# Two heads side by side in the first attention, half products, an early first load, and earlier bank hand-over in the second attention

## The reference, cut to what matters

```
first half:  n = layernorm(x); q, k, v = n @ W + b, with low-rank additions (16 heads of 16)
             routed experts: 32 experts (128 -> 128 -> 128, relu squared), 8 chosen per token, and a
             shared expert of 512; their gate gives g
first attention, per batch of 1024 tokens and per head of 16:
             softmax(q k^T / 4) v      (all 1024 keys), then @ Wo + bo; x1 = g * that + x
gate network: a ternary-weight gated network on layernorm(x1)
second attention, 32 heads of 64, rotary positions: 30 local heads (blocks of 128 queries on 192 keys,
             causal), 2 causal heads over all 1024; @ Wo + bo; times g2, plus x1
```

## Time and profile before

| | |
|---|---|
| median of 3 runs | 3305.22 us (3304.18 to 3305.37) |
| the profiled execution's own time | 3307.49 us |
| its span in the trace | 3305.7 us |
| mean granted TensorE clock | 0.982 |
| TensorE busy | 3098.8 us (94%) |
| weight loads | 2208.1 us (67%) |
| VectorE busy | 2139.0 us (65%) |
| ScalarE busy | 1854.7 us (56%) |
| POOL busy | 1111.6 us (34%) |

### The profile page before, as it was taken

The page is one execution under the profiler, slowest core; times in us unless marked ns, Lnnn a source line. Parts: engine busy times, 40 slices in busy tenths (PEclk is TensorE's granted clock), DMA queues, the critical chain, the costliest instruction groups (busy, mean ns, idle before and its releaser), DMA issues. The chain is left out here.

```text
span 3305.7 us, 62515 instructions
## 1 busy us (share of the span) xinstructions
PE 3098.8 (94%) x21586; PEld 2208.1 (67%) x21586; DVE 2139.0 (65%) x6393; ACT 1854.7 (56%) x4670; POOL 1111.6 (34%) x1753
## 2 busy tenths in 40 slices
PE   7999999979999999996987999999999999999998
PEld 5888888822333333333776888788877888778886
DVE  5776666658888888874755555555556555555555
ACT  4666666627767767673445555455554555445553
POOL 1111111010010010002015556575555655566554
PEclk9999999979999999997999999999999999999999
DMA  4111111042223132101324434354343443244432
GB/s 137 42 41 43 40 44 37 15 83 38 51 47 67 27 71 42 29 8 55 132 75 107 98 89 96 92 121 97 79 113 86 112 98 89 65 112 101 97 83 65
DMA packets 310379, 241.68 MB, mean 73 GB/s; under 512 B 150768, under 2 KB 256688, under 8 KB 309936
## 3 DMA queue, kind: packets, MB, share of 16 engines
q1 hardware_dynamic: 310064, 237.69, 29.2%
HBM read 100.71 MB, written 39.85 MB: 43 GB/s over the span
## 5 line engine op out<-in xcount | busy, mean ns | idle before, releaser
L1660 ACT ACTIVATE b_pp<-b_pp,b_nm 128x192 f32<-128x192 f32 (+2 forms) x1024 | 472.5, 463 | 458.5 <-DVE b_nm L1828 377.0
L903 DVE TENSOR_REDUCE a_mx<-ps 128x1 f32<-128x512 f32 x1024 | 636.5, 681 | 88.3 <-PE ps L851 88.2
L825 ACT ACTIVATE a_pt<-ps 128x512 f32<-128x512 f32 x1024 | 534.9, 601 | 245.1 <-PE ps L862 243.6
L1630 POOL TENSOR_SCALAR b_pp<-b_pp,b_rc 128x192 f32<-128x192 f32 x960 | 388.0, 430 | 441.1 <-DVE b_rc L1837 441.1
L1849 DVE COPY b_pt<-ps 128x384 f32<-128x384 f32 (+2 forms) x336 | 182.0, 555 | 388.1 <-PE ps L1749 369.7
L851 PE MATMUL ps<-a_k,a_q 96*128 96x512 bf16 x1024 | 399.3, 391 | 18.9 <-DMA a_k<-qk_parts 16.1
L862 PE MATMUL ps<-a_q,a_k 99*128 99x512 bf16 x1024 | 387.4, 382 | 8.9 <-issue 5.4
L1828 DVE CUSTOM_DVE_ANT_0 b_pp<-ps,b_mk 128x192 f32<-128x192 f32 x960 | 276.3, 353 | 130.8 <-PE ps L1728 130.8
L638 DVE SCALAR_TENSOR_TENSOR f_yac<-ps,f_cw,f_yac 128x128 f32<-128x128 f32 x992 | 276.6, 343 | 122.2 <-PE ps L447 120.7
L851 PEld LDWEIGHTS ps<-a_k,a_q 96*128 96x128 bf16 x1024 | 100.1, 98 | 292.1 <-issue 152.6
L447 PEld LDWEIGHTS ps<-w,f_sq 128*128 128x128 f32 x2048 | 264.9, 191 | 29.7 <-DVE f_yac L638 7.2
(11 more groups left out here) (254 smaller groups left out, 7104.3 us busy)
## 6 DMA issues: line engine op xcount, KB each, us to landing
b_rt<-b_qf SPq DMA_DIRECT2D x1024, 64.0 KB, 2.0
qk_parts<-f_aa SPq DMA_DIRECT2D x32, 384.0 KB, 2.6
a_q<-qk_parts SPq DMA_DIRECT2D x192, 64.0 KB, 3.0
a_k<-qk_parts SPq DMA_DIRECT2D x96, 128.0 KB, 5.2
v_rows<-f_va_ SPq DMA_DIRECT2D x16, 512.0 KB, 3.0
a_v<-v_rows SPq DMA_DIRECT2D x4, 2048.0 KB, 11.6
b_raw<-in_W1qT SPq DMA_DIRECT2D x64, 128.0 KB, 2.6
b_raw<-in_W1kT SPq DMA_DIRECT2D x64, 128.0 KB, 2.8
```

What stands on the lines that cost most here:

```text
L825: e.activation(pt[(4 * i + j) % 8][:, :], P.ap(s), ACT.Exp).then_inc(P.free_sem(s), 1)
L903: e.tensor_reduce(mx[kh % 3][:, j * 4 + t, h:h + 1], P.ap(s), AX.X, ALU.max, negate=True).then_inc(P.free_sem(s), 1)
L1630: m = e.tensor_scalar(x, x, r[:, 2 * u + h:2 * u + h + 1], 1.0, ALU.mult, ALU.mult)
L1660: e.activation(x, x, ACT.Exp, bias=nm[n % 4][:, c:c + 1], scale=-1.0, accum_out=sm[n % 4][:, c:c + 1]).then_inc(exp_done, 1)
```

## The change

- In the first half q and k are stored as two fp32r parts (high, low): ScalarE writes the high part with the bias, VectorE makes the low part from the bank. POOL has no part in it.
- In the first attention two heads lie side by side: one head's three stacked parts (48 rows) from partition 0, the next head's from partition 64. `max` becomes a pair of products into two neighbouring banks, read by one reduction; 32 a unit. `score` becomes a pair of products too. The maximum is added by two extra rows, made by VectorE alone. Four row transfers instead of three.
- Banks: pairs 0-1 and 2-3 for maxima and all side steps, 4 to 6 for scores, 7 for the weighted sums. There are 12 `pt` tiles.
- `pv` is split in two halves of 256 columns, of which the second is issued half a position later. Step `two` is emptied by VectorE instead of ScalarE.
- The ones in the k tiles come by six transfers. Unit 0 is loaded in the first half's last chunk, into the space of experts 0 to 15 (`ahead` step of the first half); the values have a load step of their own.
- In the second attention banks 0 and 2 are handed on at the fourth of the eight maxima. For the last batch VectorE does the gating in place of POOL.

```diff
+
+    def pair(self, step):
+        i = self.at[step][0]
+        return self.ps[:, i:i + 2, :]
...
+                if (c, e) == (NCH - 1, 14):
+                    p.append(("ahead",))
...
-                    w.wait_ge(aa2_done, m + 1)
+                    w.wait_ge(*P.emptied(("qk", c, s[2])))
                     dst = X["qk"][n, :, h * 128:(h + 1) * 128, c * CH:(c + 1) * CH].rearrange("s p t -> p s t")
-                    e.dma_start(dst, aa[m % 2][:, :, :]).then_inc(aa_out[m % 2], 16)
+                    e.dma_start(dst, aa[m % 2][:, :, :].bitcast(F32)).then_inc(aa_out[m % 2], 16)
...
+                elif k == "ahead":
+
+                    w.wait_ge(*P.filled(("up", NCH - 1, 15)))
+                    for i in range(2):
+                        w.wait_ge(aa_out[i], 16 * 2 * 2)
+                    load_unit(e, X, 0, M["q0"], M["k0"], M["q0_in"], M["k0_in"])
...
-                    w.wait_ge(r1_done, m - 1)
-                    e.activation(qf[m % 2][:, :], P.ap(s), ACT.Identity,
-                                 bias=M["bqk"][:, n, h:h + 1]).then_inc(P.free_sem(s), 1)
+                    w.wait_ge(aa_out[m % 2], 16 * (m // 2))
+                    e.activation(aa[m % 2][:, 0, :], P.ap(s), ACT.Identity,
+                                 bias=M["bqk"][:, n, h:h + 1]).then_inc(aa_high, 1)
...
-                    e.tensor_copy(aa[m % 2][:, 1, :], r1[m % 2][:, :]).then_inc(aa1_done, 1)
+                    n, h, m = s[2] // 2, s[2] % 2, 4 * c + s[2]
+                    w.wait_ge(aa_high, m + 1)
+                    e.scalar_tensor_tensor(out=aa[m % 2][:, 1, :], in0=P.ap(s), scalar=M["bqk"][:, n, h:h + 1],
+                                           in1=aa[m % 2][:, 0, :].bitcast(F32), op0=ALU.add,
+                                           op1=ALU.subtract).then_inc(P.free_sem(s), 1)
...
@@ first_attention_plan()
             emitted += 1
-            if emitted % 32 == 0:
-                out.append(("both", emitted // 32 - 1))
-                late.append((slot + (2 if slot else 0), ("rows", emitted // 32 - 1)))
+            if emitted % 16 == 0:
+                out.append(("both", emitted // 16 - 1))
+                late.append((slot + (1 if slot else 0), ("rows", emitted // 16 - 1)))
         return out
 
     p += ahead(0)
     while late:
         p.append(late.pop(0)[1])
...
+            if (u + 2) % 4 == 0:
+                p.append(("load_v", (u + 2) // 4))
+        p += ahead(2 * i + 1)
+        if i + 1 < 16 * units:
+            p.append(("score", i + 1, 0))
+        if c:
+            p.append(("pv", i - 1, 1))
+        if 2 <= c <= 5 and side:
+            p.append(side.pop(0))
+        p += ahead(2 * i + 2)
+        if i + 1 < 16 * units:
+            p.append(("score", i + 1, 1))
+        p.append(("pv", i, 0))
         if c == 7:
-            p.append(("evac", i // 8))
+            p += [("pv", i, 1), ("evac", i // 8)]
             if u % 4 == 3:
                 if i + 1 == 16 * units:
                     p += side
@@ -701,48 +706,67 @@
                 f0 = 8 * (u // 4) + 4 * h
                 for n in range(6):
                     side += [(s, f0 + n - lag) for lag, s in ((2, "three"), (1, "two"), (0, "one")) if 0 <= n - lag < 4]
-        elif 2 <= c <= 5 and side:
-            p.append(side.pop(0))
     return p + side
 
...
+    b, g = n // 4, n % 4
+    for m, parts in ((1, (0, 0, 1)), (0, (0, 1, 0))):
+        for h in range(2 if m == 0 else 1):
+            for a in range(2):
+                for r in range(3):
+                    rows = slice(64 * a + 16 * r, 64 * a + 16 * r + 16)
+                    src = X["qk"][m, parts[r], g * 64:(g + 1) * 64, b * L:(b + 1) * L].rearrange(
+                        "(p a d) t -> a d p t", p=2, a=2)[a]
+                    if m:
+                        e.dma_start(k[rows, :, :].bitcast(F32), src).then_inc(k_in, 16)
+                    else:
+                        e.dma_start(q[rows, h, :, :].bitcast(F32), src[:, :, h * CH:(h + 1) * CH]).then_inc(q_in[h], 16)
...
@@ first_attention()
             if s[0] == "max":
-                P.take(s, s[1] % 3)
+                P.take(s, 2 * (n_max % 2), 2 * (n_max % 2) + 1)
+                n_max += 1
             elif s[0] == "score":
-                P.take(s, 3 + (4 * s[1] + s[2]) % 3)
-            elif s[0] == "pv":
-                group = s[1] // 8
-                if s[1] % 8 == 0:
-                    P.take(("group", group), 6 + group % 2, fills=False)
+                for a in range(2):
+                    P.take((*s, a), 4 + n_score % 3)
+                    n_score += 1
+            elif s[0] == "pv" and s[1] % 8 == s[2] == 0:
+                P.take(("group", s[1] // 8), 7, fills=False)
             elif s[0] == "last":
                 last = 0
                 if last is None:
-                    P.take(s, 6 + (1 - group % 2 if ("group", 0) in P.at else 0))
+                    P.take(s, 2 * (n_max % 2), 2 * (n_max % 2) + 1)
+                    n_max += 1
...
+        pt = [sb(f"pt{i}", [128, CH]) for i in range(12)]
...
             w = Waits(e)
+            w.wait_ge(one_set, 1)
+            for x in ks:
+                for a in range(2):
+                    dst = x[64 * a + KS:64 * a + KX, :, :].rearrange("r j (n t) -> r (j n) t", t=128)
+                    e.dma_start(dst.bitcast(F32), spread(one[:, :], 1, 16).bitcast(F32)).then_inc(ones_in, 16)
             for s in plan:
...
+                        w.wait_ge(*P.filled(("score", 16 * (n - 3) + 15, 1, 1)))
+                    if n:
+                        load_unit(e, X, n, qs[i], ks[i], q_in[i], k_in[i])
+                elif k == "load_v":
+                    if n >= 2:
+                        w.wait_ge(pv_done, pv_at[64 * (n - 1) - 1, 1])
+                    e.dma_start(vs[n % 2][:, :, :, :].rearrange("p i h d -> p i (h d)"),
+                                X["v"][n * L:(n + 1) * L, :].rearrange("(i p) f -> p i f", p=128)).then_inc(v_in[n % 2], 16)
                 elif k == "rows":
                     i, h = n // 2 % 3, n % 2
...
+                    w.wait_ge(*P.emptied(s))
+                    for a in range(2):
+                        for r in range(2):
+                            dst = qs[i][64 * a + KS + r:64 * a + KS + r + 1, h, :, :]
+                            e.dma_start(dst.rearrange("a p (t q) -> a (p t) q", q=128).bitcast(F32),
+                                        n2[n % 2][8 * a:8 * a + 8, r, :].bitcast(F32)).then_inc(rows_in[i][h], 16)
...
                     i, j = s[1], s[2]
-                    w.wait_ge(*P.filled(s))
-                    w.wait_ge(pv_done, i - 1)
-                    e.activation(pt[(4 * i + j) % 8][:, :], P.ap(s), ACT.Exp).then_inc(P.free_sem(s), 1)
+                    if i >= 3:
+                        w.wait_ge(pv_done, pv_at[i - 3, 1])
+                    for a in range(2):
+                        w.wait_ge(*P.filled((*s, a)))
+                        e.activation(pt[(4 * i + 2 * j + a) % 12][:, :], P.ap((*s, a)),
+                                     ACT.Exp).then_inc(P.free_sem((*s, a)), 1)
                 elif k == "evac":
...
-                    e.matmul(P.ap(s), q6[u % 3][0:KS, half, j, t * 128:(t + 1) * 128],
-                             k6[u % 3][0:KS, j, h * CH:(h + 1) * CH], start=True, stop=True).then_inc(P.full_sem(s), 1)
+                    for a in range(2):
+                        r = slice(64 * a, 64 * a + KS)
+                        m = e.matmul(P.pair(s)[:, a, :], qs[u % 3][r, half, j, t * 128:(t + 1) * 128],
+                                     ks[u % 3][r, j, h * CH:(h + 1) * CH], start=True, stop=True)
+                    m.then_inc(P.full_sem(s), 1)
...
+                        w.wait_ge(*P.before((*s, a)))
+                    for a in range(2):
+                        r = slice(64 * a, 64 * a + KX)
+                        e.matmul(P.ap((*s, a)), ks[u % 3][r, j, c * 128:(c + 1) * 128], qs[u % 3][r, h, j, :],
+                                 start=True, stop=True).then_inc(P.full_sem((*s, a)), 1)
...
+                    x = slice(256 * half, 256 * half + 256)
                     for j in range(4):
-                        w.wait_ge(*P.emptied(("score", n, j)))
-                        m = e.matmul(P.ap(group)[32 * j:32 * j + 32, :], vs[b % 2][:, c, 4 * g + j, :],
-                                     pt[(4 * n + j) % 8][:, :], start=c == 0, stop=c == 7)
+
+                        w.wait_ge(*P.emptied(("score", i, j // 2, j % 2)))
+                        m = e.matmul(P.ap(group)[32 * j:32 * j + 32, x], vs[b % 2][:, c, 4 * g + j, :],
+                                     pt[(4 * i + j) % 12][:, x], start=c == half == 0, stop=c == 7 and half == 1)
                     m.then_inc(pv_done, 1)
...
-                    e.tensor_reduce(mx[kh % 3][:, j * 4 + t, h:h + 1], P.ap(s), AX.X, ALU.max,
+                    e.tensor_reduce(mx[kh % 3][:, :, jt, h], P.pair(s), AX.X, ALU.max,
```

(16 more changed lines are left out.)

172 lines of the change are left out of this document (59 added, 113 removed).

## The result

The changed kernel takes 3195.8 us in the median of four runs (3188.35 to 3204.24), the kernel before 3305.3 on the same chip: a ratio of 0.967, 95% interval 0.9645 to 0.9695. That is 110 us less, where 174 were forecast (3131). It lies inside the range given for 8 in 10 (3085 to 3215), but outside the forecast's own branch (3090 to 3180), and most of one term of the sum is missing. The profiled execution took 3204.24 us, its span is 3202.4, its mean granted clock 0.977.

The account below looks back on a forecast made before the run. TensorE's order of work was taken to bound the first attention, VectorE close behind. Gains of 96 + 15 + 60 + 3 = 174 us off 3307.5 gave 3133.5, as a median 3131; range for 8 in 10: 3085 to 3215.

Parts of the forecast that it names:

- Second attention: Projections' wait on the eighth maximum (65.3 us) goes when two banks are freed at the fourth: 60 us less, bounds 45 to 72.
- Start: Start of first attention: unit 0 loaded earlier, first score about 700.2 instead of 716.04; gain 15 us, 8 to at most 17.
- End: Last eight tiles: VectorE gates faster than POOL, 0.8 us less on each of four turns, 3 us.
- First half: q/k steps lose VectorE and POOL passes, but TensorE is the bound there: nothing, within 2 us either way.
- The loop: First attention: 2.74 us a position against 3.125 over 244 positions, 94 us, plus 2 for the last 12: 96 less.
- Pair of products: First attention: two heads' products overlap on TensorE, 0.25 us a pair, bounds 0.23 to 0.46; four pairs 1.00 a position.
- the first rival: First attention: pairs run one after the other at 0.46 us, 3.54 a position; 3327 us in all, slower; 9%.
- A half sum: First attention's weighted sum of 256 columns: 0.44 us streaming plus 0.21 entering and leaving, 0.65; bounds 0.55 to 0.75.
- The three score banks in twos: First attention: a score pair needs the previous pair's first exponential; 1.1 us a half position, under 1.3.
- Side steps, rows and coupling: First attention: 0.285 us a position for output projection and row maxima steps, plus 0.11 for TensorE's wait at "rows".
- The clock: Granted clock holds at 1.00 in the first attention's loop; the start's half clock stays; falling clock 2%.
- lockstep: First attention: the two buffers of maxima lock with side steps and split sums, about 3.0 us a position; 3196 us; 14%.

Follow-up runs that it names:

- short exponentials: The changed kernel, but from the fourth position on each exponential takes 256 queries of 512, part of the computation left out: one run of 3163.3 us.

## Why the prediction was right and where it was wrong

The time fell inside the range because the range was wide. The stretches outside the loop gave 20 us more than forecast together, the loop 90 less.

*Second attention* (-60, bounds 45 to 72). Right, a little small: 68 by the trace, 71 by itself. The wait it named went from 65.3 to 2.6 us, and most of the weight loads' wait went with it.

*Start* (-15). Right in place and size: 15.4, and 14.4 when taken back.

*End* (-3). Right: 2.8.

*First half* (0, within 2). It ended 5.4 us earlier, and the last of the experts' second products (L447) starts 7.0 us earlier (661.2, then 654.2). I said TensorE is the bound there and nothing moves. It is busy 612 of 615 us in both windows, and yet its weight loads waited for VectorE. Their waits on VectorE's sums of those products, before and then after:

```profile
PEld ps L447 <- DVE f_yac L638: 7.2, 15, 0.6
```

```profile
PEld ps L447 <- DVE f_yac L635: 0.5, 1, 0.5
```

Of the 7.0 us, 1.2 are gained ahead of the first of these products. The rest comes in small steps, 0.2 to 1.1 us at a time, at the places where the weight loads waited before. VectorE came late there and no longer does; its work fell by 13.7 us in that window and POOL's by 75.5. So the step that failed is the term put at nothing: VectorE's passes did cost TensorE time there. Which of the passes taken away gave it back was not tried.

*Between the attentions* (nothing forecast): 5.9 less. The output projection's last product starts 16.1 us behind the last sum (1479.0 to 1495.1), before 23.6 (1505.6 to 1529.2). The clock of the 54 us behind the last sum was 0.78 against 0.65, and the copy of step "two" had moved to VectorE. Which of them did it was not tried.

*The loop* (-96, range of a position 2.6 to 3.0 us). This is the step that failed. The trace's 3.00 us a position in units 1 to 14 against 2.74 forecast, term by term:

- Pair of products: 0.25 taken, 0.23 measured (1106.08 to 1106.31). The bound of full overlap was the right one, and the first rival is out.
- A half sum: 0.65 taken, bounds 0.55 to 0.75; measured 0.77 to 0.78, outside them. That is 0.57 to the next pair, and 0.09 to 0.12 more than 0.23 on each of the two steps beside it. Of it 0.44 is streaming, so a visit costs some 0.34 in entering and leaving. It is the mis-sized term: TensorE's plain position is 2.45 to 2.48 us (short exponentials) and not 2.30. The 0.21 was right for the kernel before, where plain positions take 2.85 us and 2.84 were worked out. What it could not show is the step behind the first product after a sum: 0.23 there, with products on nearly all rows, and 0.34 in the changed kernel, with pairs (1003.92 to 1004.25). In the kernel before:

```profile
790.41 0.39 PE L851 MATMUL ps<-a_k,a_q 96*128 96x512 bf16 x1
790.64 0.38 PE L862 MATMUL ps<-a_q,a_k 99*128 99x512 bf16 x1
```

The Trainium skill (TensorEngine Tiling (Array Packing), Tiling Modes) has that changing the tiling mode drains TensorE; the trace agrees, with 0.34 us for each visit to the sums from a pair and back.

- The three score banks in twos: put at 1.1 us a half position, and so at nothing in the sum. Measured 1.25 to 1.33. The exponential starts 0.43 to 0.60 behind its pair and not 0.4, and from its end to the next pair it is 0.2 to 0.28. So it was the first of the chains, 2.57 a plain position with it and 2.48 without. The answer lay in the gap left between 1.1 and the "under 1.3" beside it.
- VectorE: a reduction of 1024 taken at 1.14, 1.13 measured at the start, 1.18 in an unbroken chain. Its floor was right and did not decide.
- Side steps, rows and coupling: 0.285 + 0.11, and 0.04 more up to VectorE's floor, make 0.44 on top of 2.30. Measured 0.43 on top of 2.57, in the mean. Inside it TensorE's wait at the rows step, that I had named and not priced, is 1.0 us twice a unit.

By these the position explains 0.26 x 224 = 58 of the missing 90 us. Most of it is TensorE's own order (0.18 x 224 = 40, an estimate); the banks are the smaller part, some 16, as short exponentials gave that much in units 1 to 14 apart from the clock. Another 8 is my base: 3.125 us was the mean of 400 us with side steps, units 1 to 14 have 3.09. Unit 0 was forecast 6 us shorter and came out 11.6 longer, and the last unit's fifteen positions, forecast 3.5 shorter, came out 3.5 longer, both with half clock in them.

*The clock* ("I expect it to hold"). It did not. The changed kernel is at 1.2 GHz not only in the maxima ahead of the first score, where I had it, but up to 729 us, in a stretch where TensorE is busy 28.5 of 29 us, again from 747 to 763, and in three short dips later. A position there takes mostly 4.32 to 4.75 us. I estimate some 14 us for unit 0 (65.0 less 43.7 of unit 1; of these 21 us some 7.6 are its greater number of maxima, by 53.4 less 45.8 in the kernel before) and some 3 us for each dip (unit 4 takes 53.1 us, unit 8 with the same steps 49.8; units 10 and 6 take 50.3 and 47.0). Its four runs lie 16 us apart, the four of before beside them 2 (all runs of before together 9). The times of the four go with their mean granted clocks: 3188.35 us at 0.983, 3193.59 at 0.981, 3198.02 at 0.980, 3204.24 at 0.977. So the spread goes with the clock; why it falls in one run and not in another was not shown.

*The rivals.* The second, "lockstep", gave 3.0 us a position and 3196 us, and that is the time measured. This is luck in part: it had 31 us for the loop and 78 for the rest, and the trace has 5.6 and 97.7. Its mechanism is half right: the chains are nearly equal, but the two buffers of maxima are not what locks them (TensorE's wait for a maximum's bank is 3.3 us from 700 to 1479). The score banks are, and TensorE's visits behind them.

## What to carry to other kernels

When products for different tilings of the array alternate, price a visit by what it adds to the steps on both its sides, between products of the shapes that will stand there (0.21 us between products on nearly all rows, 0.34 between pairs), and measure a hand-over of banks as the whole round, from one start on TensorE to the next: product, signal, exponential, signal. If three such rounds come out within a tenth or two of each other, shortening one gains nothing: here some 30% to 45% of one engine's work in a plain position was taken away at a time, and the position fell by 0.09 us at most; two taken together gave 0.21. A step that waits for a result of the half position before it is best put a half position later; that was worth some 16 us with one number.

## What the runs showed that I had not expected

- Work left out made the kernel slower: with 37% of the visits to the sums gone the time rose from 3196 to 3332 us, and the granted clock fell from 0.977 to 0.911. With short exponentials beside it the same came again (3324 us, 0.903). Positions at full clock took no longer than in the changed kernel.
- The clock can stay at half while TensorE is busy 20.00 of 20 us with products of 48 and of 128 rows, and it holds 1.00 from 1000 to 1100 us of the changed kernel at 93.6 of 100 us busy. Busy time by itself did not tell which it would be.
- Two fp32r products of 512 columns on the two halves of the rows start together and take 0.23 us (1106.08 to 1106.31), as one does.
- The first pair behind a sum or a side step is slower than the others, on both its sides: the next product follows after 0.34 us instead of 0.23, and its exponential starts 0.53 to 0.60 us behind it instead of 0.43 to 0.51.
